# Folding Wv into Wo, moving a tie count into PSUM and reordering the start-up of an attention and expert kernel

## The reference

```python
xn = layernorm(x)                                     # per token
s = attn(xn)                                          # three attentions, gated, projected, normalised
g = silu(ffn(xn))                                     # 8 heads choose 16 of 1024 experts from pairs of keys
out = x + s * g

# attn, for one batch X of 512 tokens (w = which of the three attentions)
#   COMP: 128 blocks of 4 tokens, projected with Wc;  SEL: the 64 tokens with the largest score;
#   WIN: windows of 32 tokens, step 16
ctx_w = softmax((K_w Wq + bq)(K_w Wk + bk).T * scale) @ (K_w Wv + bv)
out = concat([ctx_COMP * g0, ctx_SEL * g1, ctx_WIN * g2]) @ Wo + bo
out = out * 0.5 + X * 0.5                             # X is the normalised tokens
s = (out - mean(out)) * rsqrt(var(out) + 1e-6)
```

## Time and profile before

| | us |
|---|---|
| three runs | 315.58, 316.19, 316.92 |
| median | 316.19 |
| the profiled execution, its own time | 315.58 |
| its span in the profile | 313.8 |
| start-up, to the first steady turn's attention scores | about 75 |
| one batch of four steady turns | 28.2 to 31.8 |

### The profile page before, as it was taken

How to read it: one execution, slowest core, us unless ns; L and a number is a source line. 1 busy time by engine, 2 the same in 40 slices (tenths; PEclk the granted TensorE clock), 3 DMA queues, 4 the chain that set the end, 5 groups by cost and what they waited for, 6 DMA issues and landing times.

```text
span 313.8 us, 7260 instructions
## 1 busy us (share of the span) xinstructions
PE 253.1 (81%) x1624; PEld 186.6 (59%) x1624; DVE 265.4 (85%) x1710; ACT 238.2 (76%) x1063; POOL 230.1 (73%) x351
## 2 busy tenths in 40 slices
PE   0888479759898987998888879898989798979672
PEld 0625114338576766876666667676766576758562
DVE  6586357996999899889998999898989998987555
ACT  3247325836988999699989998979899989796852
POOL 8881811115868697879798979887989798789693
PEclk9999789968999999699999999979999999799998
DMA  8910000000000000010001000100010001000102
GB/s 177 247 47 1 0 3 0 0 0 3 0 4 0 1 3 1 0 38 1 2 1 34 3 0 4 34 1 3 1 33 3 1 2 34 3 2 0 37 0 67
DMA packets 11228, 6.23 MB, mean 20 GB/s; under 512 B 1457, under 2 KB 10674, under 8 KB 11186
## 3 DMA queue, kind: packets, MB, share of 16 engines
q1 hardware_dynamic: 9858, 5.12, 6.2%
q10 hardware_dynamic: 1328, 0.66, 1.0%
HBM read 3.67 MB, written 2.10 MB: 18 GB/s over the span
## 4 chain that ended last, share of the span: by engine, by line
POOL 32%; PE 31%; issue 15%; DVE 13%; ACT 7%; POOLq 0%; DVEq 0%; ACTq 0%
POOL squareT L495 5%; POOL wgt L508 5%; PE sim L1480 3%; PE scratch L1572 3%; POOL past L480 3%; POOL wgt L516 3%; PE sim L1471 2%; DVE top L1165 2%; PE t_bank L1499 2%; POOL y L586 2%; PE s_bank L1603 2%; PE s_bank L1457 2%; POOL rstd L449 2%; POOL drop L502 2%; POOL xn_all L458 2%
## 5 line engine op out<-in xcount | busy, mean ns | idle before, releaser
L1165 DVE MAX8 top<-rest 128x8 f32<-128x40 f32 x512 | 57.1, 186 | 0.5
L1116 DVE MAX8 top<-sim 128x8 f32<-128x32 f32 x496 | 51.5, 185 | 2.7 <-PE sim L1471 2.7
L815 ACT ACTIVATE prob<-drop 128x50 f32<-128x50 f32 x232 | 53.2, 249 | 0.0
L495 POOL TENSOR_TENSOR squareT<-sideT 100x512 bf16<-100x512 bf16 x31 | 32.2, 1037 | 21.2 <-ACT sideT L730 21.2
L815 ACT ACTIVATION_READ_ACCUMULATOR prob<-drop 128x1 f32 x232 | 47.3, 206 | 0.0
L508 POOL TENSOR_TENSOR wgt<-prob,rden 128x400 f32<-128x400 f32 x30 | 25.9, 865 | 23.1 <-DVE rden L1108 23.1
L1471 PE MATMUL sim<-sim_w,xT_all 128*128 128x512 f32 x64 | 36.1, 646 | 1.4 <-ACT xT_all L764 0.8
L502 POOL TENSOR_TENSOR drop<-gap,out_by 128x400 f32<-128x400 f32 x31 | 32.6, 1051 | 5.4 <-ACT out_by L721 5.4
L480 POOL TENSOR_TENSOR past<-gap,last 128x400 f32<-128x400 f32 x31 | 26.7, 861 | 11.8 <-DVE last L1189 11.7
L1499 PE MATMUL t_bank<-gaps_of,topT 128*128 128x200 f32 x128 | 30.0, 359 | 2.2 <-ACT topT L735 2.2
L1152 DVE SCALAR_TENSOR_TENSOR spill<-n_above,rank_row 128x128 f32<-128x128 f32 x32 | 25.4, 793 | 0.0
(11 more groups left out here) (279 smaller groups left out, 789.9 us busy)
## 6 DMA issues: line engine op xcount, KB each, us to landing
out<-y_sb SPq DMA_DIRECT2D x7, 256.0 KB, 2.3
x_sb<-in_L_attn_hidden_states SPq DMA_DIRECT2D x2, 256.0 KB, 3.9
fwq_sb<-in_L_ffn_Wq ACTq DMA_DIRECT2D x2, 256.0 KB, 6.0
x_sb<-in_L_attn_hidden_states SPq DMA_DIRECT2D x1, 512.0 KB, 5.5
wc_sb<-in_L_attn_Wc SPq DMA_DIRECT2D x1, 256.0 KB
out<-last_y SPq DMA_DIRECT2D x2, 128.0 KB, 1.8
wo_in<-in_L_attn_Wo SPq DMA_DIRECT2D x1, 192.0 KB
keys_sb<-in_L_ffn_keys ACTq DMA_DIRECT2D x1, 128.0 KB, 3.4
```

The source lines that it names most:

```text
L495: nc.gpsimd.tensor_tensor(squareT[0:TWO, :], sideT[0:TWO, :], sideT[0:TWO, :], ALU.mult).then_inc(square_done, 1)
L815: last = nc.scalar.activation(prob[d][:, h, :], drop[:, h, :], ACT.Exp, scale=-1.0, accum_out=den[d][:, h:h + 1])
L1116: last = nc.vector.max(top[n % 3][:, v, 0:8], sim_bank[n % 2][:, bass.ts(v, KEYS)])
L1165: last = nc.vector.max(top[n % 3][:, v, 8:16], rest[:, v, :])
```

## The change

**Values.** Wv is transposed and multiplied with the centred Wo once, in the start-up (`turn_values`, `fold_values`, new tiles `wvT`, `wvo`, `bvo`). `values_out` and `block_values_out` then take the tokens themselves times `wvo`; units `U_VW` and `U_V` and their copies on ScalarE are gone (9 units per batch). bv times Wo gives three rows `bvo`; twelve small transfers on SP put them into `vww` as rows 80 to 82, and the window weights get three columns with the gates (`p_win`, 83 instead of 80 columns), which POOL copies in `scale_probs`. The gates are zeroed where a part has no output row.

**Residual.** `attention_out` adds the normalised tokens by the identity, two tiles in one product of 256 columns, in place of `xT_all` times `off_mean` per tile.

**Ties.** A constant tile `allowed` is put into the `sim` bank by a fifth product in `count_above`; `spill_above` adds `n_above` and that part of the bank into a third part of the bank, and `put_ties` reads it there. Each of the two has one SBUF operand left. `put_ties` comes before `mark_above`, and it now gives `sim_used`.

**Start-up.** `place_constants` stands behind the last norm group. `first_turns` on VectorE is written out: `row_stats(6)` ahead of `sum_above(0)`, `row_stats(7)` ahead of `next_8`. `expert_parts` moves behind the last logits, `top_columns(0)` and `count_above(1)` a step earlier. `centre_outputs` on ScalarE moves from batch 3 to batch 5, and the copy of `sim_w` from VectorE to ScalarE. `keep_clock` adds 32 products (6, 12, 8 and 6) on TensorE whose result nobody reads.

```diff
+            for k in range(8):
+                nc.gpsimd.memset(allowed[:, :, k:k + 1], -8.5 - k)
...
+            sp.wait_ge(bvo_done, 1)
+            for r in range(3):
+                for j in range(TB):
+                    sp.dma_start(vww[WKEYS + r:WKEYS + r + 1, j, :], bvo[:, r, :]).then_inc(bo_put, 16)
...
-                if g == 1:
+                if g == 4:
                     place_constants()
...
+                nc.gpsimd.tensor_copy(p_win[:, :, WKEYS:WROWS],
+                                      gates[:, :, :, bass.ds(b, 1)].rearrange("p g t a -> p t (g a)"))
...
-                    unit(b - 1, U_V, [(vcs[:, :], 0, bv_sb, 1.0)])
...
-                    unit(b, U_VW, [(vw[:, :], 0, bv_sb, 1.0)])
...
             def spill_above(n):
 
+                dve.wait_ge(summed_above, n + 1)
+                nc.vector.tensor_tensor(sim_bank[n % 2][:, 2 * PARTS:3 * PARTS].rearrange("p (v k) -> p v k", v=VECS),
+                                        n_above[:, :].unsqueeze(2).to_broadcast([P, VECS, 8]),
+                                        sim_bank[n % 2][:, PARTS:2 * PARTS].rearrange("p (v k) -> p v k", v=VECS),
+                                        ALU.add).then_inc(spill_done, 1)
+
+            def put_ties(n):
+
+                dve.wait_ge(spill_done, n + 1)
+                nc.vector.scalar_tensor_tensor(rest[:, :, KEYS:KEYS + 8],
+                                               sim_bank[n % 2][:, 2 * PARTS:3 * PARTS].rearrange("p (v k) -> p v k", v=VECS),
+                                               SPILL, eighth(n, 8), ALU.mult, ALU.min).then_inc(sim_used, 1)
...
-                nc.vector.scalar_tensor_tensor(spill[:, :, :], n_above[:, :].unsqueeze(2).to_broadcast([P, VECS, 8]), 2.0,
-                                               rank_row[:, 7:15].unsqueeze(1).to_broadcast([P, VECS, 8]),
-                                               ALU.mult, ALU.subtract).then_inc(spill_done, 1)
...
+            def keep_clock(count):
+
+                for _ in range(count):
+                    mm(t_bank[:, HEADS * CANDS:512], ident[:, :], ident[:, 0:512 - HEADS * CANDS], start=True, stop=True)
...
+                mm(sim_bank[n % 2][:, PARTS:2 * PARTS], ident16[:, :], allowed[:, :, :].rearrange("p v k -> p (v k)"),
+                   start=True, stop=True).then_inc(above_counted, 1)
...
+            def fold_values():
+                pe.wait_ge(bvo_done, 1)
+                mm(f_bank[:, D:4 * D], wvT[:, :], wo_sb[:, :, :].rearrange("p r d -> p (r d)"),
+                   start=True, stop=True).then_inc(values_folded, 1)
...
-                    last = mm(o[0:WKEYS, bass.ts(g, D)], vw[:, k0:k0 + WKEYS], wo_sb[:, WIN, :], start=True, stop=True)
+                    last = mm(o[0:WKEYS, bass.ts(g, D)], xT_all[:, k0:k0 + WKEYS], wvo[:, WIN, :], start=True, stop=True)
...
-                    mm(o, xT_all[:, bass.ts(b * TB + j, P)], off_mean[:, :], start=True, stop=False)
+                    if j % LAST == 0:
+                        mm(dst[:, bass.ds(j * D, LAST * D)], ident[:, :],
+                           xn_all[:, bass.ds(b * TB + j, LAST), :].rearrange("p t d -> p (t d)"), start=True, stop=False)
```

More of the change, by code:

```diff
@@ L222, in program @@
         n_above = sb("n_above", [P, VECS])
-        spill = sb("spill", [P, VECS, 8])
+        allowed = sb("allowed", [P, VECS, 8], BF16)
         topT = sb("topT", [P, 2 * P])
@@ L309, in program @@
         assert sorted([0] + POOL_NORMS + ACT_NORMS) == list(range(B))
-        M_UNITS = 11
-        (U_QW, U_KW, U_VW, U_SEL, U_COMP, U_QK, U_V,
-         U_VWW, U_VWC, U_PTW, U_PTC) = range(M_UNITS)
+        M_UNITS = 9
+        (U_QW, U_KW, U_SEL, U_COMP, U_QK, U_VWW,
+         U_VWC, U_PTW, U_PTC) = range(M_UNITS)
         def m_unit(b, k):
@@ L403, in _ @@
             nc.gpsimd.tensor_copy(ident16[:, :], ident[:, :])
-            nc.gpsimd.tensor_scalar(off_mean[:, :], ident[:, :], -1.0 / D, None, ALU.add)
+            nc.gpsimd.memset(gates[:, :, :, :], 0.0)
             nc.gpsimd.memset(neg_half[:, :], -0.5)
@@ L760, in centre_outputs @@
                 last.then_inc(wo_step, 1)
+            act.wait_ge(fold_ready, 1)
+            nc.scalar.activation(sim_w[:, :], sim_bank[1][:, :], ACT.Copy).then_inc(sim_w_done, 1)
             for b in range(B):
@@ L1012, in _ @@
             take_masks()
-            unit(0, U_VW, [(vw[:, :], 0, bv_sb, 1.0)])
             take_rank()
@@ L1030, in _ @@
             last_exps(TILES - 3)
-            unit(B - 1, U_V, [(vcs[:, :], 0, bv_sb, 1.0)])
             side_of(TILES - 1)
@@ L1245, in maxima, with first_turns @@
                                         negate=True).then_inc(max_done, 1)
-            def first_turn(n):
-                strike_above(n)
-                if n != 2:
-                    first_8(n + 1)
-                if n >= 1:
-                    gaps_of_pairs(n - 1)
-                sum_above(n)
-                if n != 2:
-                    mark_above(n + 1)
-                spill_above(n)
-                if n >= 1:
-                    gaps_of_thirds(n - 1)
-                put_ties(n)
-                if n >= 1:
-                    last_gaps(n - 1)
-                next_8(n, 0)
-                next_8(n, 1)
-                if n == 0:
-                    row_stats(6)
-                    row_stats(7)
-                if n == 2:
-                    select_tokens(3)
-                    invert_gates()
-                    mark_above(3)
-                if n == 3:
-                    invert_gate_sums()
+            def first_turns():
+                first_8(0)
+                dve.wait_ge(x_in[3], 16)
+                row_stats(4)
+                row_stats(5)
+                mark_above(0)
+                strike_above(0)
+                row_stats(6)
+                sum_above(0)
+                spill_above(0)
+                put_ties(0)
+                row_stats(7)
+                next_8(0, 0)
+                next_8(0, 1)
+                first_8(1)
+                mark_above(1)
+                strike_above(1)
+                first_8(2)
+                sum_above(1)
+                gaps_of_pairs(0)
+                spill_above(1)
+                put_ties(1)
+                mark_above(2)
+                next_8(1, 0)
+                gaps_of_thirds(0)
+                last_gaps(0)
+                next_8(1, 1)
+                strike_above(2)
+                gaps_of_pairs(1)
+                gaps_of_thirds(1)
+                last_gaps(1)
+                sum_above(2)
+                spill_above(2)
+                put_ties(2)
+                next_8(2, 0)
+                next_8(2, 1)
+                select_tokens(3)
+                invert_gates()
+                mark_above(3)
+                strike_above(3)
+                first_8(4)
+                sum_above(3)
+                spill_above(3)
+                put_ties(3)
+                mark_above(4)
+                gaps_of_pairs(2)
+                next_8(3, 0)
+                gaps_of_thirds(2)
+                last_gaps(2)
+                next_8(3, 1)
+                invert_gate_sums()
@@ L1301, in turn @@
                     next_8(n, 1)
-            first_8(0)
-            dve.wait_ge(x_in[3], 16)
-            row_stats(4)
-            row_stats(5)
-            mark_above(0)
-            for n in range(TB):
-                first_turn(n)
+            first_turns()
             for n in range(TB, TILES):
@@ L1652, in attention_out @@
                         mm(o, pT_cs[0:SELECT_K, 1, :], vwc[0:SELECT_K, 1, :], start=False, stop=False)
-                    last = mm(o, pT_win[:, j, :], vww[:, j, :], start=False, stop=True)
+                    last = mm(o, pT_win[:, j, :], vww[:, j, :], start=False, stop=(j % LAST == LAST - 1))
                 if TB - 1 in tiles:
@@ L1697, in turn @@
                     expert_weights(n - 4)
-                    project_window(b, U_VW, wv_sb)
                     count_places(n - 2)
@@ L1788, in _ @@
             scores(3)
+            expert_parts()
+            turn_values()
             top_columns(1)
@@ L1809, in _ @@
             count_above(3)
-            project_window(0, U_VW, wv_sb)
             count_ranks()
```

123 lines of the change are left out of this document (68 added, 55 removed).

## The result

The changed kernel took 313.22 us (median of four runs, 312.46 to 313.75), the one before 316.56 (four runs, 315.58 to 318.12). The ratio is 0.9888, with a 95% interval of 0.9842 to 0.9935. A second set on another occasion gave 0.9898 (0.9841 to 0.9956). So the change is faster by 1.1%, and not by the 3.2% of the forecast: 306.5 was too low by 6.7 us, and 313.2 lies outside the range.

A forecast was written before the change was run, and what follows sets the result against it. The bound was taken to be a loop POOL, TensorE, VectorE, POOL, twice a batch. From 315.6 us, -5.5 (start-up) and -3.6 (-0.59 per batch over six, first batch -0.3, tail +0.2) gave 306.5 us; range 297 to 312.5.

The forecast's parts named there:

- The start-up: Front of the kernel up to the choice of tokens, which was to begin earlier: -5.5 us.
- the term that I had put at 1.8 us at most: Start-up, ScalarE: `centre_outputs` ahead of the copy of batch 6's transposes gives back up to +1.8 us.
- The rival without a start-up gain: Choice of tokens begins at the old time, TensorE's products fill what VectorE frees: 312.0 us; chance 0.11.
- The tie step on the loop: Loop POOL, TensorE, VectorE, POOL: removing the tie step's stall, on it once a batch, frees 0.66 us per batch.
- the count's product: Fifth count product on TensorE, on both trips of a batch: 0.11 us twice, +0.2 per batch.
- POOL's copy: POOL's copy of the gates, added inside its burst: +0.2 us per batch, between 0.1 and 0.3.
- The rival in which the stall stays: Tie step still stalls, the steady part gives almost nothing, time about 310.5 us; chance 0.06.
- VectorE as the bound: Rival: the loop is only VectorE's own delay, the whole 16 us stall comes back, 294 us; chance 0.14.
- The last trip: Second trip of the loop in a batch, into the next first turn: -0.33 us for `U_V`, +0.11 for the fifth product.
- The first batch: First steady batch, which has no stall but loses its value units: -0.3 us.
- The clock: Rival: fewer TensorE products and longer waits for POOL lower its clock in more batches, about 327 us; chance 0.05.
- The price per fall: Steady batches: one fall of TensorE's clock costs a batch 1.5 us.

## Why the prediction was wrong, step by step

**The start-up: right in size, with one term too small.** Forecast -5.5, measured -5.1 at the choice of tokens and -5.4 at the first `wgt`. The statistics are over earlier, and POOL's last group starts at 23.46, not 31.38; what `centre_outputs` gives back is seen on ScalarE and TensorE.

```profile
23.46 0.24 POOL L459 TENSOR_SCALAR var<-mv 128x8 f32<-128x8 f32 x1 [1.54 <-DVE mv L1078]
```

```profile
30.60 0.30 ACT L764 ACTIVATE wo_spare<-wo_in 128x128 f32<-128x128 f32 x1
...
33.40 1.05 ACT L782 ACTIVATE xT_all<-scratch 128x512 f32<-128x512 f32 x2
```

```profile
34.02 3.41 PE L1500 MATMUL s_bank<-xT_all,zw_rows 128*32 128x512 f32 x4 [2.62 <-ACT xT_all L782]
```

```profile
12.89 1.66 DVE L1135 MAX8 top<-sim 128x8 f32<-128x32 f32 x16
...
47.14 0.66 DVE L1227 MAX8 sel_m<-z_sb 8x8 f32<-8x512 f32 x1
```

The rows are POOL's start of the last norm group, ScalarE's first instruction of `centre_outputs` and the copy behind it, TensorE's logits that waited 2.62 us for that copy and then ran at 1.2 GHz (granted clock 0.50 from 34 to 37 us), and VectorE's first instruction on tile 0 and at the choice of tokens. The wait for the copy is the term that I had put at 1.8 us at most; taken away, it gave 2.7, and the stretch at 1.2 GHz behind it came on top. That the sum came out right all the same is in part luck. The rival without a start-up gain is out.

**The tie step on the loop: right in place and size.** Forecast -0.66 with +0.11 for the count's product, measured -0.60 in that step. POOL's copy: forecast +0.2, measured +0.14 to +0.16. A PSUM operand in the place of an SBUF one costs nothing: 296 and 291 ns. An estimate from the figures of the Trainium skill ("VectorE: DVE Perf Modes", section on the TRN2 errata) would have added 65 ns to each of them; no run here shows it. TensorE's `scores` waits 0.76 us for `put_ties` in every first turn, but that is hidden, as forecast: the step into the second turn is 7.60 us before and with the tie step alone. The rival in which the stall stays is out, too.

**VectorE as the bound: out.** It lost 15.8 us of busy time and a batch lost 0.39. Most of the stall lay in time in which VectorE would have waited.

**The last trip: wrong.** I took the trip into the first turn for the same loop as the one into the third, and gave it -0.33 for `U_V` and +0.11. Measured: 8.13 before, 8.24 after. The rows show why: POOL waits there for `rden`, 1.19 us after it has already done the next `past` and `drop`,

```profile
149.10 0.86 POOL L520 TENSOR_TENSOR wgt<-prob,rden 128x400 f32<-128x400 f32 x1 [1.43 <-DVE rden L1127]
...
162.28 1.03 POOL L514 TENSOR_TENSOR drop<-gap,out_by 128x400 f32<-128x400 f32 x1
164.50 0.86 POOL L520 TENSOR_TENSOR wgt<-prob,rden 128x400 f32<-128x400 f32 x1 [1.19 <-DVE rden L1127]
```

and VectorE computes `rden` behind the sum, which stands behind the maxima, which waited for TensorE's block scores:

```profile
163.30 0.49 DVE L1258 TENSOR_REDUCE nmax<-s_bank 128x4 f32<-128x320 f32 x1 [0.80 <-PE s_bank L1663]
...
164.04 0.27 DVE L1163 TENSOR_REDUCE n_above<-sim 128x16 f32<-128x128 f32 x1
164.24 0.18 DVE L1127 RECIPROCAL rden<-den 128x8 f32<-128x8 f32 x1
```

The trip is TensorE's own work from the blocks' products to the block scores, and VectorE's order behind it. The run with the inverse early showed it. That is 0.33 too much per batch. By the table, the tie step put 0.40 on this trip instead of 0.11, and `U_V` took off 0.29 where the tie step stood and nothing where it did not. The other steps came out a little better than forecast, so that a batch at full clock lost 0.39 instead of 0.59: 1.2 us of the sum. The first batch was wrong by 0.6: forecast -0.3, measured 29.36 - 29.04 = +0.3. The values alone did give the 0.3 there (28.74); the tie step alone took 0.6 (29.67), where there was no stall to lose.

**The clock: the step that failed.** I made the sum at the clock of before, and dismissed the other case with a chance of 0.05 because batches at full clock hold long waits on TensorE already, and the units removed are few. The second holds: in a batch at full clock TensorE's busy time went from 26.17 to 25.70 us. The first misread its rows: the 4 us are the sum of all idle times of a batch, 30.30 - 26.17. Its longest single one was 1.39 us, and behind that came the window values' product:

```profile
157.76 0.32 PE L1541 MATMUL c_bank<-ident,wgt 128*100 128x128 f32 x1 [1.39 <-POOL wgt L523]
157.91 0.62 PE L1565 MATMUL scratch<-xT_all,wv_sb 128*128 128x272 f32 x2
158.85 0.20 PE L1525 MATMUL f_bank<-count_s,sideT 101*128 101x100 bf16 x1 [0.31 <-POOL squareT L495]
```

So these rows held no single wait of 4 us, and could not show that more short ones do no harm. The price per fall was right, 1.5 us in the forecast and 31.70 - 29.88 = 1.8 measured. What all falls together take was not. In the profiled executions both kernels have three slow batches, but two of those of before stand at 0.95 and all three of the changed kernel at 0.89, and its tail is at 0.76. The seven batches of the changed kernel lost 214.8 - 209.0 = 5.8 us and its tail 1.6. Those of before lost some 3.6 (three of its batches took 31.9, 31.2 and 31.4 us instead of some 30.3), and its tail nothing. The term left out is 5.8 + 1.6 - 3.6 = 3.8 of the 6.0 us by which the profiled execution, 312.5, missed the forecast; most of the rest is the last trip and the first batch. With the clock held in both kernels the difference is 9.1 us, the forecast's own sum, but that is in part luck: the seven batches gave 2.7 instead of 3.8, and the start-up 7.0 instead of 5.5 between two executions of which only one had the stretch around 35 us.

**Open** stays why the clock falls in one batch and not in the next one, whose rows read the same, why it fell for so long ahead of the steady turns with the tie step alone, why the first `wgt` is 1.8 us late there even with the steady clock held, and what keeps the two falls at 123 and 273 us with the window product back.

## What to carry to other kernels

Where TensorE runs near full use with short waits, a change that takes work from it, or shortens its partners, has to be costed twice: at the clock of before, and with one more slow stretch per period. Short products that nobody reads, in the waits, tell the two apart in one run, and in the changed kernel they were worth more (7.4 us) than the change itself (3.3). And each wait of a period needs its own releaser: two waits of one engine for one tile were held by two different chains.

## What the runs showed of the hardware that was not expected

178 unread products of 128 columns made a kernel 7.4 us faster in the stretches where they stand (5.8 in the seven batches, 1.6 in the tail) and lengthened no batch (29.86 against 29.88). In one execution the clock went to 1.2 GHz behind a turn in which no single idle time of TensorE was over 0.8 us (0.71, 0.77, 0.49), and in three other batches with the same idle times it did not; with 0.33 in the place of 0.77 it went down in two of seven batches instead of four. An idle time of 2.62 us in the start-up was followed by a stretch at 1.2 GHz in six of seven profiles. Removing a stall of 16 us of VectorE and nothing else made the kernel 1.1% slower, and no different from its like when the clock was held in the steady turns (314.0 us both, the mean of ten runs each).
